# Routing tokens to experts by lists scattered during the conditioning stage, in a fused adapter and mixture-of-experts kernel

## The chip, the cores and the metric

The kernel runs on 1 core of one Trainium2 chip. The metric is the device time of the program in microseconds (us). TensorE (PE), VectorE (DVE), ScalarE (ACT), GpSimd (POOL) and SyncE (SP) each have an instruction queue of their own that runs in order; semaphores couple them. SP starts the plain DMAs, POOL the indirect ones.

## What is computed

4096 tokens of 512 numbers (64 sequences of 64). Each passes a linear layer with a low-rank adapter chosen by its sequence, then two shared experts and the best 2 of 16 routed ones.

```python
def cond(x, W, A, Bm, scalings, adapter_idx):            # x: 64, 64, 512
    H = einsum('btd,od->bto', x, W)
    xa = einsum('btd,brd->btr', x, A[adapter_idx])       # rank 16, 8 adapters
    return H + einsum('btr,bor->bto', xa, Bm[adapter_idx]) * scalings[adapter_idx][:, None, None]

def ffn(x, Wsh_up, Wsh_down, Wrt_up, Wrt_down, W_router):
    xt = x.reshape(B * S, H)
    shared = sum over 2 experts of gelu(xt @ up) @ down  # 512 -> 256 -> 512
    probs = softmax(xt @ W_router)                       # 16 experts
    top_v, top_i = top_k(probs, 2)
    gate = sum(one_hot(top_i) * top_v)
    routed = sum over 16 experts of (gelu(xt @ up) * gate) @ down
    return shared + routed

out = x + ffn(cond(x))
```

## The kernel before

The tokens go in 16 chunks of 256 (NC), each of two tiles of 128 (NT). Where a product is not done in fp32 as it stands, both operands are scaled by powers of two, split into an fp16 part and an fp16 remainder ("high" and "low"), and three fp16 products are summed. Each scale needs the largest magnitude of a tensor over all partitions: DVE reduces along the row, POOL across partitions (`partition_all_reduce`, L517 for weights, L523 for x).

**Conditioning.** One PE step per chunk c (`cond_step`, L1278): adapter products of c (L1238), linear products of tile 0 (L1249), transposes of the conditioned chunk c-1 (L1265), linear products of tile 1, router logits of c-1 (L1274), second adapter products of c (L1257). Chunks 0 and 1 are multiplied whole in fp32 (`whole=True`), since the scales aren't there yet; chunks 2 to 15 use splits: ACT makes the high part of chunk c+1 (`high_x`, L674), DVE the low part (`x_low`, L964). DVE also takes the maximum of the conditioned rows (L898), of the next x (`x_largest`, L947), and the best two logits (`top`, L881). In chunks 1 to 7 DVE searches the 16 lots of expert weights for their maxima as SP loads them (`lot_maxima`, L906: three lots a step in chunks 2 and 3, two later); in steps 4 and 5 it also splits the shared weights. In chunks 8 to 15 ACT and DVE split the weights of two experts a step (`high_routed` L648, `low_routed` L937, both through L641 and L935). SP loads x of chunk c+3 in the step of chunk c, then stores the conditioned rows and their transposes; the loads of further weight lots stand in the same queue behind waits for `lot_max_ready` (`weights_chunk`, L368).

**Sort.** After the last chunk, DVE builds one-hot rows of all 32 tiles (L1051), PE sums them over partitions (`prefix_products`), DVE adds them up over tiles (L1063, L1064), counts tiles per expert, and works out every token's place (L1083 to L1093). The list of tokens by place is found by 64 small matmuls (`inversion_products`, L1313) over one-hot operands which DVE writes two at a time (`places`, L1107 and L1108), in 8 groups. `tok` (L1119) signals `sorted_ready`; only then can POOL gather rows (L574).

Between these stand, in PE's queue, the up and down products of the first 6 chunks of the shared experts (`shared_up` L1327, `shared_down` L1340), in an order written out by hand (L1344 to L1368). Their low parts are made by POOL (`low_condT` L542, `low_hid` L547) from a copy that ACT has scaled a second time (L664, L769). The order ends in the transposes of the first gathered rows, `shared_down(2, 1)`, and the first routed product (`r_up(0)`, L1433).

**Routed stage.** 79 tiles of 128 slots, a pipeline over tiles (`r_round`): transposes, up, down, results stored to `r_dram`. **Late stage.** The other 10 chunks of the shared experts, while POOL gathers back the two routed rows of each token (L608) and DVE weighs and adds them.

Of the kernel before, what the change touches and what calls it, by code (L numbers as in the profile page):

```python
# [5 lines left out]
F32 = mybir.dt.float32  # L6
# [34 lines left out]
GRP = 8  # L41
NG = TT // GRP * K_TOP
# [12 lines left out]
assert EARLY == NC - EARLY - 4 and EARLY <= A_HALF and NC % 4 == 0 and NC == E_RT and EM == HK and NG == 8  # L55


def adaln_moe_kernel(nc, xT, x_rows, idx, WT, AT, BmT, scal, sh_up, sh_dn, rt_w, w_r, out):
# [17 lines left out]
    with ctx:  # L76
# [13 lines left out]
        s_dram = nc.dram_tensor("s_dram", [TOK, H], F32, kind="Internal").ap()  # L90
        r_dram = nc.dram_tensor("r_dram", [NJ * P, H], F32, kind="Internal").ap()
        c_dram = nc.dram_tensor("c_dram", [P], F32, kind="Internal").ap()
# [11 lines left out]
        w_place, a_place = 13, 14  # L104
# [47 lines left out]
        acc0, acc1, pref = carve([((TT, E_RT), F32)] * 3)  # L152

        inv_bufs = carve([((GRP, P), F16), ((GRP, NJ_ALL), F16)] * 2)
        in_part, in_val = inv_bufs[0::2], inv_bufs[1::2]

# [11 lines left out]
        def routed_row(slot, r, t):  # L168
# [8 lines left out]
        iota_p = sb("iota_p", [P, P], F16)  # L177
        iota_j = sb("iota_j", [P, NJ_ALL], F16)
# [11 lines left out]
        lg_c = [sb(f"lg_c{s}", [P, NT, E_RT]) for s in range(2)]  # L190
# [6 lines left out]
        words = TT * E_RT // 2  # L197
        oh = [arena[:, r * words:(r + 1) * words].bitcast(BF16).rearrange("p (t e) -> p t e", t=TT) for r in range(K_TOP + 1)]
        oh_sum = oh.pop()
        at = (K_TOP + 1) * words  # L200
        hi_i, lo_i, hi_f, lo_f = [arena[:, at + n * K_TOP * TT:at + (n + 1) * K_TOP * TT].bitcast(I32 if n < 2 else F32)
                                  .rearrange("p (r t) -> p r t", r=K_TOP) for n in range(4)]
# [5 lines left out]
        pos_f = sb("pos_f", [P, K_TOP, TT])  # L208
        pos = sb("pos", [P, K_TOP, TT], I32)
        past = sb("past", [P, E_RT])  # L210
        tile_col = sb("tile_col", [P, 1])
        tile_e = sb("tile_e", [1, NJ_ALL // 2, 4], I32)
# [7 lines left out]
        expo = sb("expo", [P, len(SCALED)], I32)  # L220
# [7 lines left out]
        x_max = [sb(f"x_max{s}", [P, 1]) for s in range(2)]  # L228
        x_max_all = [sb(f"x_max_all{s}", [P, 1]) for s in range(2)]
# [6 lines left out]
        c_all_row = xam[0][:, 0:P]  # L236

        def col(v, n):
            return v[:, n:n + 1]

# [5 lines left out]
        PRE, TOT, INV, TILE_E = bank[6], bank[7], bank[0], bank[5]  # L246
# [5 lines left out]
        lot_max_ready, largest_ready, reduced, scale_ready, un_ready = (  # L252
            sem("lot_max_ready"), sem("largest_ready"), sem("reduced"), sem("scale_ready"), sem("un_ready"))
# [7 lines left out]
        x_max_found, x_max_ready, x_reduced = sem("x_max_found"), sem("x_max_ready"), sem("x_reduced")  # L261
# [9 lines left out]
        onehot_ready, prefix_ready = sem("onehot_ready"), sem("prefix_ready")  # L271
        shifted_ready, exp_ready = sem("shifted_ready"), sem("exp_ready")
        tile_col_ready, tile_row_ready = sem("tile_col_ready"), sem("tile_row_ready")
        place_ready, place_used, sorted_ready = sem("place_ready"), sem("place_used"), sem("sorted_ready")
# [16 lines left out]
        c_all_stored, c_all_spread = sem("c_all_stored"), sem("c_all_spread")  # L291
# [45 lines left out]
        def _(sp):  # L337
            sp.dma_start(at_in, AT).then_inc(w_adapters, 16)
            sp.dma_start(flat(act_in[0][:]), chunk_T(xT, 0)).then_inc(act_loaded[0], 16)
            sp.dma_start(sc_col[:], scal).then_inc(w_mask, 16)  # L340
            sp.dma_start(idx_b[:], idx.partition_broadcast(P)).then_inc(w_mask, 16)
            for dst, src in ((w_in, WT), (bmt, BmT), (wr, w_r)):
                sp.dma_start(dst, src).then_inc(w_cond, 16)
            sp.dma_start(flat(act_in[1][:]), chunk_T(xT, 1)).then_inc(act_loaded[1], 16)
# [7 lines left out]
            def cond_chunk(i, s, more=True, first=False):  # L352
                c = 2 * i + s
                if more:
                    if first:
                        sp.wait_ge(act_used, 2)
                    else:
                        sp.wait_ge(x_split, c)
                    sp.dma_start(flat(act_in[1 - s][:]), chunk_T(xT, c + 3)).then_inc(act_loaded[1 - s], 16)
                sp.wait_ge(rows_ready, NT * c + NT)  # L360
                sp.dma_start(chunk_rows(xc_dram, c), rows[s][:]).then_inc(rows_stored[s], 16)
                sp.wait_ge(condT_ready, NT * c + NT)
                sp.dma_start(chunk_T(xcT_dram, c), flat(hid[s][:])).then_inc(condT_stored[s], 16)


            def weights_chunk(i, s):
                cond_chunk(i, s, first=(i == 0 and s == 0))
                for r in (2 * s, 2 * s + 1):  # L368
                    n = 4 * i + r
                    if n + 5 == w_place:  # L370
                        sp.wait_ge(act_used, 2)
                        sp.wait_ge(lin_split, 2)
# [28 lines left out]
            load_x(0)  # L401
            cond_chunk(A_HALF - 1, 1, more=False)
            sp.wait_ge(largest_ready, 4)
            sp.dma_start(c_dram.rearrange("(p o) -> p o", o=1), col(largest, C_ALL)).then_inc(c_all_stored, 16)
            sp.wait_ge(c_all_stored, 16)
            sp.dma_start(c_all_row, c_dram.partition_broadcast(P)).then_inc(c_all_spread, 16)
# [8 lines left out]
            sp.wait_ge(cond_ready, TT)  # L415
            for c in range(2):
                next_condT(c)
# [76 lines left out]
        def _(pool):  # L494
# [5 lines left out]
            iota(iota_p[:], P)  # L500
            iota(iota_j[:], NJ_ALL)
            iota(iota_e[:], E_RT)
            nc.gpsimd.iota(tok_no[:], [[P, TT]], base=-TOK // 2, channel_multiplier=1,
# [4 lines left out]
            pool.wait_ge(masks, 3)  # L508
# [5 lines left out]
            def reduce_max(n, a, b):  # L514

                pool.wait_ge(largest_ready, n)
                nc.gpsimd.partition_all_reduce(largest_all[:, a:b], largest[:, a:b], P, RMAX).then_inc(reduced, 1)  # L517

            def x_reduce(c, s):
                pool.wait_ge(x_max_ready, c - 1)
                nc.gpsimd.partition_all_reduce(x_max_all[s][:], x_max[s][:], P, RMAX).then_inc(x_reduced, 1)  # L523

            reduce_max(1, LIN_W, SH_UP)
            reduce_max(2, SH_UP, RT_UP)
            pool.wait_ge(scale_ready, 1)
            for c in range(2, NC):
                x_reduce(c, c % 2)
                if c == NC // 2 + 1:  # L530
                    reduce_max(3, RT_UP, C_ALL)
# [8 lines left out]
            def low_condT(c):  # L540
                pool.wait_ge(condT_half, c + 1)
                nc.gpsimd.tensor_tensor(actT[c % 2][:, 1], by_block(early_condT(c)), actT[c % 2][:, 0],  # L542
                                        ALU.subtract).then_inc(actT_ready, 1)

            def low_hid(c):
                pool.wait_ge(hid_half, c + 1)
                nc.gpsimd.tensor_tensor(hidT[c % 2][:, 1], by_block(tmp[:]), hidT[c % 2][:, 0],  # L547
# [959 lines left out]
```

## Time and profile before

| | us |
|---|---|
| median of 3 runs | 679.23 |
| lowest, highest | 679.11, 682.99 |
| profiled execution, its own time | 681.92 |
| its span | 679.9 |
| PE busy | 627.5 (92%) |
| DVE busy | 457.4 (67%) |
| ACT busy | 327.2 (48%) |
| POOL busy | 222.6 (33%) |

The span runs from the first to the last instruction; the execution's own time has 2.0 us more around it. PE's busy time is modelled, so the order of its pieces and what it waits for say more than its share. "L12" is line 12 of the kernel. In a row of groups the numbers after the bar are total busy us and mean ns of one, then the idle time just before it and what ended that.

### The profile page before, as it was taken

To read this page: it belongs to the slowest core of one execution; us is meant where nothing else is said; L and a number is where in the kernel's file an instruction comes from. 1 tells how busy PE (TensorE), PEld (TensorE's weight loads), DVE (VectorE), ACT (ScalarE), POOL (GpSimd) and SP (SyncE) were. 2 spreads that over 40 slices of the span, in tenths; PEclk is the share of its full clock that TensorE was granted. 3 is DMA by queue.
4 is the path that set the end of the run, shared out by engine and by line. 5 is a ranking of instruction groups with operands and counts; after the bars stand their busy time and mean duration, and the time that the engine had idled before them with its cause. 6 is when DMAs were issued, how large, how long until landed. Compare 5 with 4: busy or idle time off the path is not lost.

```text
span 679.9 us, 13742 instructions
## 1 busy us (share of the span) xinstructions
PE 627.5 (92%) x4115; PEld 428.4 (63%) x4117; DVE 457.4 (67%) x900; ACT 327.2 (48%) x480; POOL 222.6 (33%) x288
## 2 busy tenths in 40 slices
PE   4998999999989758889999999999999999989794
PEld 2465656566657435556777777777777777665561
DVE  2779999999974998525555555555555554688674
ACT  1333224677775743464555555555555554333230
POOL 1000000101012742373333333333333306777771
PEclk9997999999998988999999999999999999999898
DMA  7688994343334312165555555555555539989966
GB/s 275 281 312 286 374 346 168 123 157 142 132 127 128 124 63 93 32 217 171 159 159 169 161 154 159 164 168 157 156 159 167 164 107 377 366 301 362 369 205 248
DMA packets 49765, 135.68 MB, mean 200 GB/s; under 512 B 6160, under 2 KB 6288, under 8 KB 47312
## 3 DMA queue, kind: packets, MB, share of 16 engines
q1 hardware_dynamic: 38304, 97.93, 39.1%
q0 software_dynamic: 11440, 37.50, 20.0%
q8 instruction: 11, 0.18, 0.1%
q14 instruction: 10, 0.08, 0.0%
HBM read 86.38 MB, written 49.02 MB: 199 GB/s over the span
## 4 chain that ended last, share of the span: by engine, by line
PE 53%; DVE 17%; POOL 12%; issue 7%; DMA 7%; ACT 1%; SPq 0%; DVEq 0%; POOLq 0%; ACTq 0%
PE bank L1412 15%; PE bank L1393 14%; POOL rtw L608 9%; PE bank L1249 7%; PE bank L1377 5%; DVE lot_max L906 5%; DMA act_in<-xT 3%; PE bank L1402 2%; PE bank L1327 2%; PE bank L1257 2%; PE bank L1274 2%; DMA region<-xc_dram,slot_idx 2%; PE bank L1238 1%; DVE x_max L947 1%; PE bank L1265 1%
## 5 line engine op out<-in xcount | busy, mean ns | idle before, releaser
L1129 DVE SCALAR_TENSOR_TENSOR region<-bank,scale,region 128x512 f16<-128x512 f32 x79 | 59.2, 751 | 128.7 <-ACT region L809 128.7
L1393 PE MATMUL bank<-rtw,region 128*128 x948 | 116.4, 273 | 0.0
L1412 PE MATMUL bank<-rtw,tmp 128*128 x474 | 115.2, 379 | 0.6 <-DVE tmp L1137 0.6
L1393 PEld LDWEIGHTS bank<-rtw,region 128*128 128x128 f16 x948 | 92.8, 98 | 10.1
L1340 PE MATMUL bank<-shw,hid 128*128 128x512 f16 x384 | 91.3, 397 | 8.3 <-DVE rtw L1193 7.7
L574 POOL DMA_INDIRECT region<-xc_dram,slot_idx x79 | 77.1, 976 | 61.3 <-POOL slot_idx L571 61.3
L1327 PE MATMUL bank<-act_in,shw 128*128 128x256 f16 x768 | 89.4, 277 | 2.9 <-ACT tmp L756 1.7
L1327 PEld LDWEIGHTS bank<-act_in,shw 128*128 128x128 f16 x768 | 75.8, 100 | 16.0 <-ACT tmp L756 2.2
L816 ACT ACTIVATE region<-bank,un_dn 128x512 f32<-128x512 f32 x79 | 54.3, 687 | 57.3 <-PE bank L1412 54.8
L608 POOL DMA_INDIRECT rtw<-r_dram,row_idx x64 | 70.0, 1093 | 27.6 <-issue 14.8
L1340 PEld LDWEIGHTS bank<-shw,hid 128*128 128x128 f16 x384 | 38.4, 102 | 56.4 <-issue 10.0
L1412 PEld LDWEIGHTS bank<-rtw,tmp 128*128 128x128 f16 x474 | 46.3, 98 | 39.2 <-issue 1.3
L805 ACT ACTIVATE tmp<-bank,un_up 128x256 f32<-128x256 f32 x79 | 37.4, 473 | 60.2 <-PE bank L1393 60.2
L1168 DVE SCALAR_TENSOR_TENSOR rtw<-rtw,gate 128x512 f32 (+1 forms) x64 | 45.4, 750 | 15.2 <-DMA rtw<-r_dram,row_idx 13.0
L809 ACT ACTIVATE region<-bank,scale 128x512 f16<-128x512 f32 x79 | 54.1, 687 | 2.2 <-PE bank L1377 2.2
L523 POOL PARTITION_ALL_REDUCE x_max_all<-x_max x14 | 10.7, 763 | 134.9 <-DVE x_max L949 134.9
L1377 PE MATMUL bank<-ident,region 128*128 128x128 f32 x316 | 47.4, 273 | 2.6 <-DMA region<-xc_dram,slot_idx 2.5
L571 POOL COPY slot_idx<-tok 128x1 int32 (+1 forms) x79 | 14.4, 182 | 106.5 <-PE bank L1377 97.0
L756 ACT ACTIVATE tmp<-bank,un_up 128x256 f32<-128x256 f32 x44 | 20.4, 471 | 52.2 <-PE bank L1327 49.9
L641 ACT ACTIVATE rtw<-rtw,scale 128x1024 f16<-128x1024 f32 (+1 forms) x32 | 35.8, 1152 | 17.3 <-DVE rtw L935 15.1
L935 DVE SCALAR_TENSOR_TENSOR rtw<-rtw,scale 128x1024 f16<-128x1024 f32 x32 | 39.6, 1279 | 4.4 <-ACT rtw L641 4.3
L1135 DVE TENSOR_SCALAR tmp<-bank,to_mid 128x256 f16<-128x256 f32 x79 | 38.2, 484 | 6.1 <-PE bank L1402 2.7
(157 smaller groups left out, 910.0 us busy)
## 6 DMA issues: line engine op xcount, KB each, us to landing
r_dram<-region SPq DMA_DIRECT2D x79, 256.0 KB
rtw<-rt_w SPq DMA_DIRECT2D x16, 1024.0 KB, 7.4
act_in<-xT SPq DMA_DIRECT2D x16, 512.0 KB, 3.8
xc_dram<-rows SPq DMA_DIRECT2D x16, 512.0 KB, 3.7
xcT_dram<-hid SPq DMA_DIRECT2D x16, 512.0 KB, 2.8
rtw<-x_rows SPq DMA_DIRECT2D x16, 512.0 KB, 5.4
rtw<-xcT_dram SPq DMA_DIRECT2D x13, 512.0 KB, 6.1
out<-rtw SPq DMA_DIRECT2D x9, 512.0 KB, 5.6
```

Of the source, the lines that this page charges most:

```text
L574: nc.gpsimd.indirect_dma_start(out=xg[s], out_offset=None, in_=xc_dram, in_offset=bass.IndirectOffsetOnAxis(ap=slot_idx[s][:].bitcast(U32) ...
L608: nc.gpsimd.indirect_dma_start(out=routed_row(slot, r, t), out_offset=None, in_=r_dram, in_offset=bass.IndirectOffsetOnAxis(ap=row_idx[slo ...
L809: nc.scalar.activation(xgT[s][:, 0], R_XT[s][:].rearrange("p (k t) -> p k t", k=HK), ACT.Copy, scale=col(scale, C_ALL).bitcast(F32)).then_ ...
L816: nc.scalar.activation(rrow[s], R_DN[s][:], ACT.Copy, scale=col(un_dn, ROUTED)).then_inc(rrow_ready, 1)
L1129: nc.vector.scalar_tensor_tensor(xgT[s][:, 1], R_XT[s][:].rearrange("p (k t) -> p k t", k=HK), col(scale, C_ALL).bitcast(F32), xgT[s][:, 0 ...
L1168: last = nc.vector.scalar_tensor_tensor(y, routed_row(slot, r, t), gate[:, r, bass.ds(c * NT + t, 1)], y, ALU.mult, ALU.add)
L1249: last = mm(COND[NT * s + t][:], act_in[s][:, k, at] if whole else xp[s][:, ap, k, at], w_in[:, k, :] if whole else wt[:, bp, k, :], start ...
L1327: last = mm(UP[em % 2][:, 0:CHUNK], shw[:, e, w0:w0 + P], actT[s][:, xp, k, :], start=(k == 0 and n == 0), stop=(k == HK - 1 and n == 2))
L1340: last = mm(DOWN[t][:], hidT[s][:, xp, em, t * P:(t + 1) * P], shw[:, em // DM, w0:w0 + H], start=(em == 0 and n == 0), stop=(em == EM - 1 ...
L1377: last = nc.tensor.transpose(R_XT[s][:, k * P:(k + 1) * P], xg[s][:, k * P:(k + 1) * P], ident[:])
L1393: last = mm(R_UP[s][:, 0:D], xgT[s][:, xp, k, :], rtw[:, bass.ds(e, 1), w0:w0 + D].rearrange("p a d -> p (a d)"), start=(k == 0 and n == 0 ...
L1412: last = mm(R_DN[s][:], midT[s][:, xp, m, :], rtw[:, bass.ds(e, 1), w0:w0 + H].rearrange("p a h -> p (a h)"), start=(m == 0 and n == 0), s ...
```

## The change

1. **Ranks during conditioning.** `top` now also makes the one-hot rows of its chunk. POOL (`count`) adds up one-hot rows of earlier chunks per partition; PE (`rank_products`) sums them over partitions behind the router's products; DVE (`list_places`, chunk c-2 in step c) reads each token's rank within its expert and forms a slot in a list of 4096 per expert; POOL scatters the token numbers into the lists in DRAM, 4 indirect DMAs of 128 numbers of 4 bytes a chunk (`scatter`, chunk c-3 in step c). The lists are cleared at the start by a DMA of 256 KB.
2. **After the last chunk** DVE only counts tiles, POOL gathers the used pieces of the lists with one indirect DMA, PE transposes them, DVE writes `tok`. The places for the way back (`pos`) are found later. The 64 matmuls with their operands, the prefix sums over tiles, and the two small DMAs for the last maximum are gone.
3. **Maxima over partitions by TensorE.** DVE writes the identity times the column of maxima (`x_diag`, `diag`), PE multiplies ones by it (`spread`, `spread_x`, one matmul of 128 columns each), DVE reduces the 128 columns. For x of chunk c+2 the matmul stands in step c in front of the router's products, which so wait for `x_largest(c+2)`; `x_scales(c+2)` reads it once the logits are there, and stands behind all the step's lots.
4. **Low x on GpSimd.** ACT makes the high part and then scales x in place; POOL subtracts (`low_x`).
5. **One whole fp32 chunk** (chunk 0). Chunk 1 is split and waits for the scales.
6. **Early low parts on DVE.** `low_condT` and `low_hid` of chunks 0 to 6 move from POOL to DVE, straight from the unscaled source; ACT's second scaled copies go.

```diff
@@ sync
+            for c in range(1, 3):
+                sp.dma_start(flat(act_in[c % 2][:]), chunk_T(xT, c)).then_inc(act_loaded[c % 2], 16)
+            sp.wait_ge(masks, 5)
+            sp.dma_start(lists.rearrange("(p a) n -> p (a n)", p=P), lg[:].rearrange("p t e -> p (t e)")).then_inc(lists_cleared, 16)
             sp.dma_start(arrived(0), sh_up).then_inc(w_shared, 16)
             sp.dma_start(spare, sh_dn).then_inc(w_shared, 16)
-            sp.wait_ge(act_used, 1)
-            sp.dma_start(flat(act_in[0][:]), chunk_T(xT, 2)).then_inc(act_loaded[0], 16)
...
@@ gpsimd
+            def low_x(c, s):
+                pool.wait_ge(x_half, c)
+                nc.gpsimd.tensor_tensor(un_cond[s][:], x_unscale[s][:].bitcast(F32), col(unscale, LIN_W).bitcast(F32), ALU.mult)
+                nc.gpsimd.tensor_tensor(xp[s][:, 1], act_in[s][:], xp[s][:, 0], ALU.subtract).then_inc(x_split, 1)
...
+            low_x(1, 1)
+            pool.wait_ge(lists_cleared, 16)
+            for c in range(1, NC):
+                if c + 1 < NC:
+                    low_x(c + 1, (c + 1) % 2)
+                if c > 2:
+                    scatter(c - 3)
+                count(c - 1, (c - 1) % 2)
+            scatter(NC - 3)
+            count(NC - 1, 1)
+            scatter(NC - 2)
+            scatter(NC - 1)
+            pool.wait_ge(list_ready, 1)
+            pool.wait_ge(scattered, 16 * K_TOP * TT)
+            nc.gpsimd.indirect_dma_start(
+                out=tokT, out_offset=None, in_=lists,
+                in_offset=bass.IndirectOffsetOnAxis(ap=list_i[:].bitcast(U32), axis=0),
+            ).then_inc(tokT_loaded, 16)
...
@@ vector, a step of chunks 2 to 7 (x_low has left the steps of 8 to 15 too, which end in the same three calls)
-            def search_step(i, s, lots, masked=False):
+            def search_step(i, s, lots):
                 c = 2 * i + s
-                if not masked:
-                    mask_xa(c, s)
+                mask_xa(c, s)
                 row_max(c - 1, 1 - s)
-                x_low(c + 1, 1 - s)
...
+                x_largest(c + 2, s)
+                for at in lots:
                     lot_maxima(at)
                 x_scales(c + 2, s)
-                for at in lots[2:] if masked else lots[1:]:
-                    lot_maxima(at)
                 top(c - 1, 1 - s)
+                list_places(c - 2, s)
...
@@ vector, behind the last chunk
+            link(nc.vector.tensor_reduce(col(largest, C_ALL), c_chunk[:], AX_X, ALU.max))
+            spread_out(C_ALL, C_ALL + 1)
+            early_low_condT(1)
+            early_low_hid(0)
+            find_all(C_ALL, C_ALL + 1)
             top(NC - 1, 1)
...
+            list_places(NC - 2, 0)
+            early_low_condT(2)
+            scales(4, C_ALL, C_ALL + 1)
+            result_scales(SH_REST, C_ALL, SH_UP, SH_DN)
+            result_scales(ROUTED, C_ALL, RT_UP, RT_DN)
+            early_low_hid(1)
+            list_places(NC - 1, 1)
...
+            early_low_condT(3)
+            early_low_hid(2)
             dve.wait_ge(tile_row_ready, 1)
...
+            dve.wait_ge(inverted, 1)
+            nc.vector.tensor_copy(tok[:], INV[:, 0:NJ_ALL]).then_inc(sorted_ready, 1)
+            early_low_condT(4)
+            early_low_hid(3)
...
@@ tensor
+            def rank_products(k, s):
+                pe.wait_ge(counted, k + 1)
+                mm(PLACE, lower[:], oh_sum[s][:], start=True, stop=False)
+                return mm(PLACE, ones[:], earlier[s][:], start=False, stop=True)
...
+                if peaks_of is not None:
+                    pe.wait_ge(x_all_found, peaks_of - 1)
+                    spread_x(peaks_of)
+                if ranks_of is not None:
...
+                    rank_products(ranks_of, 1 - s)
...
             shared_up(0, 0, first=True)
-            router_products(NC - 1, 1)
+            pe.wait_ge(logit_copied, NC - 1)
+            spread(4, 1)
+            router_products(NC - 1, 1, ranks_of=NC - 2)
             shared_up(0, 1)
-            prefix_products()
+            last_rank_products()
             shared_down(0, 0, first=True)
             shared_up(1, 0)
             tile_expert_product()
             shared_down(0, 1)
+            token_transpose()
             shared_up(1, 1)
-            inversion_products(0)
...
```

## Rows read from the trace of the kernel before

**Rows 1.** The page's chain that ended last: shares by engine, by line.
```profile
PE 53%; DVE 17%; POOL 12%; issue 7%; DMA 7%; ACT 1%; SPq 0%; DVEq 0%; POOLq 0%; ACTq 0%
PE bank L1412 15%; PE bank L1393 14%; POOL rtw L608 9%; PE bank L1249 7%; PE bank L1377 5%; DVE lot_max L906 5%; DMA act_in<-xT 3%; PE bank L1402 2%; PE bank L1327 2%; PE bank L1257 2%; PE bank L1274 2%; DMA region<-xc_dram,slot_idx 2%; PE bank L1238 1%; DVE x_max L947 1%; PE bank L1265 1%
```

**Rows 2.** Stretches: busy us (count) by engine, granted clock, DMA share, GB/s.
```profile
133.60:187.90 54.30, 54.30 (x323) 34.84 (x321) 52.40 (x116) 40.76 (x48) 5.42 (x5) 1.00 0.37 138
202.60:296.30 93.70, 76.41 (x526) 49.65 (x526) 67.50 (x201) 50.41 (x70) 39.52 (x24) 0.90 0.32 102
250.00:262.00 12.00, 8.40 (x41) 3.78 (x42) 9.51 (x35) 1.85 (x4) 3.27 (x2) 0.63 0.00 0
296.30:553.20 256.90, 253.72 (x1865) 189.95 (x1864) 133.49 (x232) 140.92 (x234) 91.77 (x153) 1.00 0.55 162
```

**Rows 3.** Timeline: where steps 2, 4, 8, the first shared and routed products start.
```profile
16.55 2.62 ACT L668 ACTIVATE region<-rtw,scale 128x2048 f16<-128x2048 f32 x2 [14.46 <-DVE scale L920]
...
37.00 0.27 PE L1238 MATMUL bank<-tmp,region 128*128 128x256 f16 x1
...
64.55 0.27 PE L1238 MATMUL bank<-tmp,region 128*128 128x256 f16 x1
...
110.14 0.27 PE L1238 MATMUL bank<-tmp,region 128*128 128x256 f16 x1
...
202.63 0.40 PE L1327 MATMUL bank<-act_in,shw 128*128 128x256 f16 x1
...
296.30 0.93 PE L1393 MATMUL bank<-rtw,region 128*128 x7
```

**Rows 4.** The chain in order of time, one PE step (start, us, what).
```profile
133.61 1.31 PE bank L1238 x12
134.92 2.59 PE bank L1249 x12
137.51 0.87 PE bank L1265 x8
138.38 2.59 PE bank L1249 x12
140.97 1.69 PE bank L1274 x16
142.66 1.81 PE bank L1257 x4
```

**Rows 5.** Groups of instructions by line, whole span.
```profile
L906 DVE TENSOR_REDUCE lot_max<-rtw 128x2 f32<-128x2048 f32 x16 | 36.3, 2278 | 0.0
L947 DVE TENSOR_REDUCE x_max<-act_in 128x1 f32<-128x1024 f32 x14 | 17.0, 1213 | 6.1 <-DMA act_in<-xT 6.1
L964 DVE SCALAR_TENSOR_TENSOR tmp<-act_in,x_scale,tmp 128x1024 f16<-128x1024 f32 x7 | 8.9, 1277 | 0.0
L674 ACT ACTIVATE tmp<-act_in,x_scale 128x1024 f16<-128x1024 f32 x7 | 8.0, 1147 | 17.6 <-DVE x_scale L958 17.6
L914 DVE TENSOR_REDUCE largest_all<-xam 128x1 f32<-128x128 f32 x1 | 0.3, 285 | 0.0
L893 DVE CAST chosen<-best_i_c 128x4 f32<-128x4 uint32 x16 | 4.6, 284 | 0.5
```

**Rows 6.** Timeline: GpSimd's subtraction beside small VectorE instructions.
```profile
200.36 2.13 POOL L542 TENSOR_TENSOR act_in<-tmp,act_in 128x1024 f16<-128x1024 f32 x1 [25.34 <-ACT tmp L664]
200.51 2.00 DVE L893 CAST chosen<-best_i_c 128x4 f32<-128x4 uint32 x1
```

**Rows 7.** GpSimd's indirect DMAs, one line: ns min/median/max.
```profile
L608 POOL DMA_INDIRECT rtw<-r_dram,row_idx x64: 942/966/1886, 562.9 to 664.0; - x64
```

**Rows 8.** DMA issues by line: KB each, us to landing.
```profile
sc_col<-scal SPq DMA_DIRECT2D x1, 0.5 KB, 3.3
c_dram<-largest SPq DMA_DIRECT2D x1, 0.5 KB, 10.2
```

**Rows 9.** Timeline at the end of the sort.
```profile
281.86 0.24 DVE L1119 TENSOR_SCALAR tok<-bank 128x80 int32<-128x80 f32 x1 [0.26 <-PE bank L1313]
```

More of the change, by code:

```diff
@@ new lines, in scatter @@
+            def scatter(k):
+                pool.wait_ge(slot_ready, k + 1)
+                for r in range(K_TOP):
+                    for n in range(NT * k, NT * k + NT):
+                        nc.gpsimd.indirect_dma_start(
+                            out=lists.rearrange("a (n o) -> (a n) o", o=1),
+                            out_offset=bass.IndirectOffsetOnAxis(ap=pos[:, r, n:n + 1].bitcast(U32), axis=0),
+                            in_=tok_no[:, n:n + 1], in_offset=None,
+                        ).then_inc(scattered, 16)
@@ new lines, in _ @@
+            early_low_condT(4)
+            early_low_hid(3)
+            dve.wait_ge(scattered, 16 * K_TOP * TT)
+            for r in range(K_TOP):
+                link(nc.vector.tensor_tensor(acc, iota_e[:].unsqueeze(1).to_broadcast([P, TT, E_RT]),
+                                             chosen[:, r, :].unsqueeze(2).to_broadcast([P, TT, E_RT]), ALU.is_equal))
+                link(nc.vector.tensor_tensor(acc, acc, start_s[:].unsqueeze(1).to_broadcast([P, TT, E_RT]), ALU.mult))
+                link(nc.vector.tensor_reduce(starts[:, r, :], acc, AX_X, ALU.add))
@@ L1127, in low_xgT @@
+            nc.vector.tensor_tensor(pos[:], starts[:], rank[:], ALU.add).then_inc(pos_ready, 1)
+            early_low_condT(5)
+            early_low_hid(4)
+            link(nc.vector.tensor_tensor(lg[:], lg[:], best[:, :, 0:1].to_broadcast([P, TT, E_RT]), ALU.subtract))
+            nc.vector.tensor_tensor(best[:, :, 1:2], best[:, :, 1:2], best[:, :, 0:1], ALU.subtract).then_inc(shifted_ready, 1)
+            early_low_hid(5)
+            early_low_condT(6)
             def low_xgT(j, s):
@@ L1294, in _ @@
             pe.wait_ge(lin_split, 2)
[L1295 to L1304 removed]
+            adapter_inputs(1, 0, 1)
@@ new lines, in _ @@
+            cond_products(1, 1, 0, first=True)
+            cond_transposes(0, 0, first=True)
+            cond_products(1, 1, 1, first=True)
+            pe.wait_ge(x_all_found, 2)
+            spread(2, 2)
+            router_products(0, 0, peaks_of=3, first=True)
+            adapter_products(1, 1)
+            pe.wait_ge(all_found, 2)
+            cond_step(2, 1, 0, second=True)
+            cond_step(3, 1, 1)
+            with pe.Fori(2, A_HALF // 2) as i:
+                for s in range(2):
+                    cond_step(2 * i + s, i, s)
@@ new lines, in _, with last_rank_products @@
+            for s in range(2):
+                cond_step(NC // 2 + s, A_HALF // 2, s, middle=s == 0)
+            with pe.Fori(A_HALF // 2 + 1, A_HALF - 1) as i:
+                for s in range(2):
+                    cond_step(2 * i + s, i, s)
+            for s in range(2):
+                cond_step(NC - 2 + s, A_HALF - 1, s, more=False)
+            cond_transposes(NC - 1, 1)
+            def last_rank_products():
+                pe.wait_ge(logit_copied, NC)
+                pe.wait_ge(all_found, 4)
+                pe.wait_ge(rank_read, NC - 1)
+                rank_products(NC - 1, 1)
+                mm(TOT, ones[:], earlier[1][:, 1, :], start=True, stop=False)
+                mm(TOT, ones[:], oh_sum[1][:, 1, :], start=False, stop=True).then_inc(ranked, 1)
```

476 lines of the change are left out of this document (233 added, 243 removed).

## The prediction

> **What bounds the kernel now.** I read the page's chain first [rows 1]: PE's two routed products are its largest lines, but DVE has 17% of it, and POOL's and the lots' lines stand there too, so the stages have different limits. The stretches say where [rows 2]. The routed stage, 296.30 to 553.20, is PE throughout at full clock; the change leaves its loop as it is, and the late stage too. The stretch before it, 202.60 to 296.30, holds the sort: PE is busy 76.41 of 93.70 us at a granted clock of 0.90, and in 250 to 262 the clock is 0.63 of 2.4 GHz, that is, part of it at the 1.2 GHz level, after PE had stood idle for DVE. In the conditioning steps of 133.6 to 187.9 PE is full, and DVE is nearly so (52.40 of 54.30). So the question is by how much the first routed product, at 296.30 [rows 3], moves; everything behind it moves along. That product stands at the end of a fixed order on PE, which begins at 202.63.
>
> **Part 1: the sort behind the last chunk (what goes).** Half a shared chunk, up or down, is 48 products of 256 columns or 24 of 512, the same column count. Twelve products of 512 columns take 2.59 us in an undisturbed step [rows 4], so half a chunk takes 5.2. In PE's new order stand 12 halves before `r_up(0)`: 62.4 us. To these come the last router products (1.7), 8 transposes of gathered rows (0.9, as the eight at 137.51), and about 1.6 for the new small products and the first gelu, on which the third block of the first half waits: 66.6 us. Now it is 93.7. The difference, 27, is what PE loses to DVE's writing of one-hot operands, to POOL's low parts and to the lower clock.
>
> Does the rest keep up? With U for the start of the first half: ACT needs for a chunk four gelus, a high hidden part, a high input and two row copies, under 6 us of 10.4. `top(15)` ends near U+10, for the router stands behind the first half and DVE first makes two low parts of 1.28 (L964's shape [rows 5]). The second half ends at U+12.9, `last_rank_products` at U+13.2; `list_places(15)` is held back by `early_low_hid(1)` to U+17. The scatters of the last chunk are four indirect DMAs at 1.0 us [rows 7] and their semaphore time: issued by U+22. DVE's twenty or so small links give the list numbers at about U+21. Scatter landed at U+25, gather issued and landed at U+29. PE reaches `token_transpose` behind the second chunk's first down half, at U+29.0: a dead heat, against `tok` at 281.86 now [rows 9], which is U+79. DVE's low parts for chunks 3 to 5 then come 2 to 5 us ahead of PE. I add 2 us for small stalls: 68.5 instead of 93.7, **-25.2 us**.
>
> The scatter is the unknown here; this trace has none. Nearest are: issue 966 ns, up to 1886 [rows 7]; landing 3.3 us for 128 elements of 4 bytes when little is under way, 10.2 us for such a store behind four transfers of 512 KB [rows 8]. I take 3.5 and 4 us for scatter and gather, since at U+22 the queues are light (mean DMA share 0.32 in that stretch [rows 2]). With 10.2 for the scatter and 6 for the gather, `tok` is 9 us later, and so is PE.
>
> **Part 2: the head.** The first scales are ready at 16.5 (ACT's first split [rows 3]). Now chunk 1's maximum, three diagonals and a round trip over PE stand before them: some 2.7 us, 19.2. ACT splits the linear weights (2.62), makes chunk 1's high part and scales it in place, 2 times 1.15 [rows 5], 24.1; POOL subtracts, 2.13 [rows 6], after DVE's split of the linear weights: 27.2. PE, done with chunk 0 before that, waits. Step 1 as fp16 then takes 7.4 us to its router (1.31+2.59+0.87+2.59 [rows 4]), 34.6. The router now needs chunk 3's diagonal, and DVE has in front of it the row maximum (1.2, the shape of L947), the two shared weight maxima (2 times 2.28 [rows 5]) and the maximum itself (1.21): 37.1. Router 1.7 and adapter 1.8 end at 41.0. Step 2 started at 37.00 [rows 3]: **+4.0**. What the fp16 products of chunk 1 save on fp32 is in this, since it starts late anyway.
>
> **Part 3: steps 2 to 7.** DVE sets the pace: from step 4 to step 8 it is 45.6 us, 11.4 a step [rows 3], over PE's 10.9 [rows 4]. It loses `x_low`, 1.28, and its scalar, hardly anything from start to start (1.3 in all), and gains the diagonal (0.25 and a link of 0.2), the reduction of 128 columns (0.285 [rows 5] and 0.17 for the link), and three links of `list_places`, 0.8; `top` loses three copies and gains a wider comparison, even. Net 0.4 a step (small DVE links by estimate: 0.17 for the instruction, as the undisturbed casts of rows 5, and as much again for the semaphore), and I take 0.55, as the order puts the lots ahead of `x_scales`, and the next x load stands on SP behind a wait for them: 6 steps, **+3.3**. Step 8 starts at 117.5 instead of 110.14.
>
> **Part 4: steps 8 to 15.** At step 8 PE waits in its own queue for three diagonals of the routed scales, which DVE can only write after step 7, 2.7 us; before, DVE alone stood for that. I take **+2.1**. Then PE is full: one product of 128 columns and two of 32 a step, at 0.1 us each, as the sixteen of 16 columns in 1.69 [rows 4]: 6 steps, **+1.7**. DVE comes to 10.5 (52.40 in five steps [rows 2]) - 1.3 + 1.7 = 10.9 us, just under PE's 11.1. At the end ACT has one scaled copy less before the last rows: **-1.0**.
>
> **Part 5: the shared port.** While POOL's subtraction ran (2.13 us), DVE's cast of 4 elements took 2.00 us [rows 6]; the other 15 took 0.17 ((4.6 - 2.0)/15 [rows 5]). There are 15 `low_x` in the new conditioning. By my placing, `low_x(c+1)` runs 3.8 to 6.0 us into step c, when DVE is at its two row maxima. These have one input, and that they aren't held up is assumed, not shown. So most of it is hidden: 0.16 us a chunk, **+2.4**. The bounds are 0 and 2.13 a chunk.
>
> The Trainium skill says why ("SBUF — State Buffer", section "SBUF: two separate sides"): the port pair that VectorE and GpSimd share is an exclusive lock for the whole instruction, which a VectorE instruction takes with two SBUF inputs against a GpSimd one that reads SBUF. The trace agrees, 2.00 us against 0.17. By that rule alone `low_routed`, with two inputs, would be held up each time it meets `low_x`: this speaks against the change, and is the first rival.
>
> **The sum.** Conditioning: 4.0 + 3.3 + 2.1 + 1.7 - 1.0 + 2.4 = +12.5. Sort: -25.2. Together -12.7: the profiled execution's 681.92 would be 669.2, and the median of the runs, 679.23, which stands 2.7 under it, becomes **666.5 us**. That is 1.9% less; a measurement of this kernel can tell about 1% (6.8 us) from no change.
>
> **Rivals.**
> *The port eats it (slower; 0.12).* `low_x` lies not under the reductions but across `low_routed` and `low_shared`. For it: DVE is at 97% in steps 9 to 14 [rows 2], so nothing else hides it. Against it: ACT's high parts come after cond_T there, and DVE has to wait for them anyway. The full price is 15 times 2.13, 32 us, in place of my 2.4: 696. It turns the change slower from 1.0 us a chunk on (12.7/15 more than I took).
> *The lists come late (0.13).* Landings as in the upper bound: +9, 675.5; what speaks for it is the store of 10.2 us. If each scatter's issue costs 1.9 us, as the longest of rows 7, POOL, with 2.3 for `low_x`, 4 times 2.2 and by estimate 1.6 for `count` a step, is over PE's 11.1 by 1.6 a step and comes to about the same range, 685 (within this chance).
> *Conditioning hardly pays (0.20).* DVE's added links fall into waits for loads (L947 waited 6.1 us for x [rows 5]) and for ACT; only the head's 4 us stay: 666.5 - 8.5 = 658.
> *The sort wasn't what held PE.* Then nothing is gained and +12.5 stays: 692; PE's order shows no other reason for 17 idle us, so 0.03.
> The forecast itself: 0.52.
>
> **Range and chances.** 8 in 10 lie between 653 (conditioning free, sort -26.5) and 682. Faster by over 1% (under 672.4): my case and the third rival, with part of the second, 0.79. Within 1%: 0.09. Slower by over 1%: 0.12.
>
> **What would show it.** Right: step 2's first product near 41, step 8's near 117, the first shared one near 215, `tok` some 30 us after that, `r_up(0)` near 283.5, granted clock 1.00 in between, steps of 11.1 to 11.3 us in 9 to 15. Wrong: DVE instructions of about 2 us beside L-lines of `low_x` in steps 8 to 15 (first rival); PE idle before the token transpose (second); steps over 11.5 us with POOL at over 10 busy. If the token list is there before U+25 and still `r_up(0)` is later than U+70, DVE's new low parts are late, a step that I costed at 2 us.

## The result, and the profile after

The changed kernel takes **707.75 us** (median of 4 runs, 701.67 to 716.01) against 679.49 for the kernel before beside it: ratio 1.0374, 95% interval 1.0275 to 1.0473. It is slower, outside the range of 653 to 682. The ratio leaves out the longest of the four runs, 716.01 us, which is in the slow state; it is the profiled one (span 714.3), and without it the median is 704.32, so that differences taken from 707.75 below would be 3.4 us smaller.

Where the stages begin, first and last start in us, as the lines' own view of the changed kernel gives them (L1281 is the adapter product that opens a step, L1418 the first shared product, L1476 the first routed one); they answer to [rows 3]:

```profile
L1281 PE MATMUL bank<-tmp,region x84: 272/273/307, 40.3 to 228.1; 128*128 128x256 f16 x84
L1418 PE MATMUL bank<-act_in,shw x768: 272/273/421, 251.0 to 696.6; 128*128 128x256 f16 x192
L1476 PE MATMUL bank<-rtw,region x948: 272/273/273, 332.2 to 589.2; 128*128 x190
```

Step 2 starts at 40.3, 0.7 us from the forecast, so the head is as worked out. But the first shared product comes at 251.0 instead of 215, and `r_up(0)` at 332.2 instead of 283.5. Conditioning lost 48.4 us against before (forecast 12.5); the sort stage takes 81.2 us instead of 93.7 (forecast 68.5). Everything behind is as it was.

Stretches of the changed kernel (busy us and count of PE, PEld, DVE, ACT, POOL; granted clock, DMA share, GB/s; the last two are the stages of [rows 2]):

```profile
80.00:100.00 20.00, 3.30 (x18) 3.25 (x18) 5.02 (x5) 0.00 (x0) 1.89 (x2) 0.54 1.05 122
82.00:95.00 13.00, 0.00 (x0) 0.00 (x0) 0.09 (x1) 0.00 (x0) 0.19 (x1) 0.50 1.17 126
120.00:140.00 20.00, 12.96 (x55) 8.25 (x54) 8.38 (x22) 4.08 (x6) 6.03 (x10) 0.66 1.06 141
251.00:332.20 81.20, 71.49 (x469) 47.70 (x466) 32.77 (x86) 37.79 (x58) 31.20 (x35) 0.89 0.56 132
332.20:589.00 256.80, 254.45 (x1872) 190.60 (x1871) 134.61 (x235) 141.73 (x235) 89.79 (x152) 1.00 0.54 160
```

From 82 to 95 the compute engines stand all but still and the 16 DMA engines are full, at 126 GB/s (the view's share can pass 1, since it counts a packet's whole time where the packet starts). The kernel before had the same fullness in 80 to 100, at three times the rate:

```profile
80.00:100.00 20.00, 18.57 (x107) 11.53 (x106) 19.73 (x39) 5.93 (x9) 0.35 (x1) 1.00 0.94 363
```

So the DMA engines are as busy while they move a third of the bytes. The page's part on DMA of the changed kernel (packets, MB, share of 16 engines; KB each, us to landing):

```profile
q1 hardware_dynamic: 38160, 98.12, 49.2%
xc_dram<-rows SPq DMA_DIRECT2D x16, 512.0 KB, 8.9
xcT_dram<-hid SPq DMA_DIRECT2D x16, 512.0 KB, 7.3
act_in<-xT SPq DMA_DIRECT2D x15, 512.0 KB, 8.8
lists<-tok_no,pos POOLq DMA_INDIRECT x64, 8.7
```

and of the kernel before:

```profile
q1 hardware_dynamic: 38304, 97.93, 39.1%
act_in<-xT SPq DMA_DIRECT2D x16, 512.0 KB, 3.8
xc_dram<-rows SPq DMA_DIRECT2D x16, 512.0 KB, 3.7
xcT_dram<-hid SPq DMA_DIRECT2D x16, 512.0 KB, 2.8
```

The plain transfers are the same in number and size, and take over twice as long. Who waits for them? The waits of the changed kernel between 40 and 200 us (us in total, times, longest), and the timeline around the first long stop:

```profile
DVE x_max L989 <- DMA act_in<-xT: 44.9, 6, 19.2
PE bank L1313 <- DVE tile_e L994: 36.6, 5, 17.7
```

```profile
77.39 1.00 POOL L541 DMA_INDIRECT lists<-tok_no,pos  x1 [0.15 <-issue]
...
79.03 0.91 SPq L361 DMA_DIRECT2D act_in<-xT  x1
...
81.23 0.96 POOL L541 DMA_INDIRECT lists<-tok_no,pos  x1 [0.30 <-issue]
94.91 1.22 DVE L989 TENSOR_REDUCE x_max<-act_in 128x1 f32<-128x1024 f32 x1 [19.19 <-DMA act_in<-xT]
```

Four scatters of 512 bytes each (L541) are issued from 77.4 to 82.2; an x chunk is issued among them at 79.0, behind two weight lots of 1 MB, and lands at 94.9; DVE's row maximum (L989) starts only then, and behind it the diagonal, the router on PE and the whole step. The chain that ended last has such transfers too. Its three longest:

```profile
68.00 26.89 DMA act_in<-xT
...
126.12 24.79 DMA act_in<-xT
...
251.81 22.12 DMA xcT_dram<-hid
```

The last of the three is the store of the last conditioned chunk's transposes (their buffer is called `hid`). The next load waits for it on SP, ACT waits for that load, and PE stops at 283.9 in the third shared chunk:

```profile
283.94 5.30 PE L1418 MATMUL bank<-act_in,shw 128*128 128x256 f16 x24 [4.17 <-ACT tmp L771]
```

An earlier stop of 5.5 us, up to 263.9, comes from a load that is late in the same way (ACT waits 7.1 us for `rtw<-xcT_dram`, DVE for ACT, PE for DVE). These two stops are 9.7 us of the sort stage. None of the four rivals names this. The list is late too (GpSimd's gather waits 5.9 us for the last scatter), but that stands behind the 35 us that are lost by then. What is left is that the scatters slow the core's other transfers, or that the order of the loads does it. The experiments take these apart.

### The profile page after: what moved, and what is told of

The parts are those of the page before. It is cut to its first block, busy times and chain, and to the rows that moved or that the text cites. A ratio compares the mean times of both kernels' runs of the same rounds, so it can differ in the third digit from the quotient of the medians.

```text
span 714.3 us, 13732 instructions
## 1 busy us (share of the span) xinstructions
PE 637.6 (89%) x4120; PEld 435.1 (61%) x4121; DVE 423.9 (59%) x805; ACT 331.9 (46%) x483; POOL 303.2 (42%) x432
## 3 DMA queue, kind: packets, MB, share of 16 engines
q1 hardware_dynamic: 38160, 98.12, 49.2%
## 4 chain that ended last, share of the span: by engine, by line
PE 57%; DMA 17%; POOL 9%; issue 7%; DVE 6%; ACT 2%; SPq 1%; POOLq 0%; DVEq 0%; ACTq 0%
PE bank L1495 14%; PE bank L1476 14%; DMA act_in<-xT 10%; POOL rtw L622 8%; PE bank L1292 5%; PE bank L1460 5%; PE bank L1300 3%; PE bank L1339 3%; PE bank L1418 3%; DMA xcT_dram<-hid 3%; PE bank L1431 3%; PE bank L1281 3%; PE bank L1485 2%; DMA rtw<-r_dram,row_idx 1%; DVE x_max L989 1%
## 5 line engine op out<-in xcount | busy, mean ns | idle before, releaser
L1476 PE MATMUL bank<-rtw,region 128*128 x948 | 116.4, 273 | 0.0
L1418 PE MATMUL bank<-act_in,shw 128*128 128x256 f16 x768 | 91.8, 282 | 9.7 <-DVE act_in L1094 5.5
L1476 PEld LDWEIGHTS bank<-rtw,region 128*128 128x128 f16 x948 | 92.7, 98 | 10.1 <-issue 0.2
L1431 PE MATMUL bank<-shw,hid 128*128 128x512 f16 x384 | 88.8, 389 | 8.2 <-DVE rtw L1236 8.2
L1418 PEld LDWEIGHTS bank<-act_in,shw 128*128 128x128 f16 x768 | 77.3, 101 | 24.0 <-DVE act_in L1094 5.6
L541 POOL DMA_INDIRECT lists<-tok_no,pos x64 | 65.8, 1027 | 21.3 <-issue 16.4
L817 ACT ACTIVATE tmp<-bank,un_up 128x256 f32<-128x256 f32 x79 | 37.5, 474 | 61.0 <-PE bank L1476 61.0
L699 ACT ACTIVATE rows<-bank,un_cond 128x512 f32<-128x512 f32 x30 | 20.4, 685 | 84.2 <-PE bank L1300 83.8
L1292 PE MATMUL bank<-region,arena 128*128 128x512 f16 x192 | 45.1, 386 | 0.0
L989 DVE TENSOR_REDUCE x_max<-act_in 128x1 f32<-128x1024 f32 x15 | 18.2, 1214 | 45.0 <-DMA act_in<-xT 44.9
```

Source lines behind the costliest of these rows:

```text
L541: nc.gpsimd.indirect_dma_start(out=lists.rearrange("a (n o) -> (a n) o", o=1), out_offset=bass.IndirectOffsetOnAxis(ap=pos[:, r, n:n + 1]. ...
L1292: last = mm(COND[NT * s + t][:], x_first[:, k, at] if whole else xp[s][:, ap, k, at], w_in[:, k, :] if whole else wt[:, bp, k, :], start=( ...
L1418: last = mm(UP[em % 2][:, 0:CHUNK], shw[:, e, w0:w0 + P], actT[s][:, xp, k, :], start=(k == 0 and n == 0), stop=(k == HK - 1 and n == 2))
L1431: last = mm(DOWN[t][:], hidT[s][:, xp, em, t * P:(t + 1) * P], shw[:, em // DM, w0:w0 + H], start=(em == 0 and n == 0), stop=(em == EM - 1 ...
L1476: last = mm(R_UP[s][:, 0:D], xgT[s][:, xp, k, :], rtw[:, bass.ds(e, 1), w0:w0 + D].rearrange("p a d -> p (a d)"), start=(k == 0 and n == 0 ...
```

## The experiments

All ratios stand against the kernel before on the same chip, whose medians in the three groups of runs were 681.54 (e1 to e4), 681.46 (e5, e7, e8, e9) and 682.10 us (e6, e10, e11, e12). The edits are shown shortened.

### Without the scatters, and beside the kernel before

```diff
 e1:
-  nc.gpsimd.indirect_dma_start(out=lists..., in_=tok_no[:, n:n + 1])
-  pool.wait_ge(scattered, 16 * K_TOP * TT)
-  nc.vector.tensor_copy(tok[:], INV[:, 0:NJ_ALL])
+  nc.vector.tensor_scalar(tok[:], INV[:, 0:NJ_ALL], part_f[:], None, ALU.add)
 e4, e5, on the kernel before, in GpSimd's loop behind x_reduce(c), c from 2:
+  for n in range(4):
+      nc.gpsimd.indirect_dma_start(out=lists, in_=tok_no[:, n:n + 1],
+          index place_i[:, 4 * c - 8 + n])
 e4: place_i[p, j] = 128 * j + p      e5: place_i[p, j] = j + 64 * p
 both: GpSimd waits for all 56 scatters behind the loop
```

> The changed kernel without its 64 scatters; the token list is filled with partition numbers instead, so each routed tile gathers rows 0 to 127, and the routing list is not computed; all other instructions stay. Theory S (the scatters slow the core's plain DMAs in the conditioning): the median lands of the x chunks and of the stored rows are back near those of the kernel before (3.8 and 3.7 us instead of 8.8 and 8.9), the first shared product starts near 215 us instead of 251, and the total is 662 to 672 us. Rival O (the order of the loads, the wait of SP, or the shared port cost the time, and the scatters are innocent): x still lands late, the first shared product stays beyond 240, total over 695 us.

Measured: **662.94 us**, ratio 0.9726 (0.9695 to 0.9756). First shared product at 216.9, `r_up(0)` at 283.1. The stored rows land as before (median 3.3 us); the x chunks do not come back to 3.8 us, as I had expected, but only to 6.3.

> The kernel before plus 56 scatters, four a chunk from chunk 2 on, each 128 numbers of 4 bytes into 128 neighbouring places of a scratch array; nothing waits for them before the first shared sum. Theory S: the conditioning loses 15 to 45 us, x lands at 7 us or more, total 695 to 725 us. Rival O: POOL has room for four issues of 1 us a chunk, total within 3 us of the kernel before (677 to 683).

Measured: **752.32 us**, ratio 1.1011 (1.0952 to 1.1071), beyond my 725. 28 KB in 56 scatters cost 70.8 us in a kernel that has nothing else of the change. Its page:

```profile
q1 hardware_dynamic: 38304, 97.93, 51.2%
rtw<-rt_w SPq DMA_DIRECT2D x16, 1024.0 KB, 18.3
act_in<-xT SPq DMA_DIRECT2D x16, 512.0 KB, 16.3
```

> The kernel before plus the same 56 scatters of 128 numbers as in e4, but each number 256 bytes from the next one of its scatter. Theory N (neighbours written within one scatter stall the core's transfers): within 4 us of the kernel before, 678 to 686 us, x chunks landing at 4 to 5 us (median). Rival A (any 4-byte write does it, where it goes plays no part): as e4, over 740 us.

Measured: **683.17 us**, ratio 1.0031 (1.0003 to 1.0059): 1.7 us. Its page:

```profile
q1 hardware_dynamic: 38304, 97.93, 39.4%
rtw<-rt_w SPq DMA_DIRECT2D x16, 1024.0 KB, 7.4
act_in<-xT SPq DMA_DIRECT2D x16, 512.0 KB, 4.5
```

Here, as DMAs, bytes, POOL's work and issue times are alike, the places of the 4-byte writes decide between 70.8 us and 1.7. One more thing stands in e5: its four scatters of a chunk write four neighbouring places for each partition, and by the end all 64 places of each 256 bytes are written. Neighbours that *successive* scatters write do no harm that shows; those of one and the same scatter do.

### How far apart, how wide

```diff
 e2: out=wide (rows of 16 floats), in_=iota_e[:]           64 bytes a write
 e3: pos * 16     e6: pos * 8     e7: pos * 2              4 bytes a write, 64, 32, 8 bytes apart
 all: tok[:] is filled with partition numbers
```

> The changed kernel, whose 64 scatters write 64 bytes per token instead of 4 into a scratch array of 4 MB (the list stays as cleared and the token list is filled with partition numbers). Same number of DMAs, of descriptors and of issues; only the size and spacing of each write differ. If it is the small size of a write (4 bytes, neighbours in one 64-byte line or not): as without scatters, total 662 to 675 us. If it is the number of descriptors or the way an indirect DMA goes (software queue, 128 rows each): as the changed kernel, over 695 us, x landing at 8 us or more.

> The changed kernel, whose 64 scatters write their 4 bytes per token 64 bytes apart in a scratch array of 4 MB (one more small DVE instruction a chunk; the token list is filled with partition numbers). If neighbouring 4-byte writes of different DMA engines into one line are what stalls: as without scatters, 662 to 675 us. If any 4-byte write stalls, wherever it goes, or any indirect DMA: as the changed kernel, over 695 us.

> As e3 and e7, with the places 32 bytes apart (4-byte writes; the token list is filled with partition numbers). Between 8 bytes (683.1) and 64 bytes (666.8). If the unit in which neighbours stall is 32 bytes or less: 664 to 669 us. If it is 64 bytes, two places share a unit: 670 to 678 us.

> As e3, but the places are 8 bytes apart instead of 64 (as for these runs, the token list is filled with partition numbers). Theory N with a unit of 64 bytes or more: still several numbers of one expert in a unit, so most of the loss stays, 690 to 710 us. If only writes that touch within a few bytes count: as e3, about 667 us.

Measured: e2 **666.73 us** (ratio 0.9792, 0.9759 to 0.9826), e3 **666.76** (0.9764, 0.9703 to 0.9825), e6 **667.43** (0.9804, 0.9752 to 0.9855), e7 **683.08** (1.0014, 0.9991 to 1.0038). The number of writes is that of the changed kernel in all four, and so are the issues: neither 64 indirect DMAs nor 4-byte writes as such cost more than 5 us over e1. In e7 a loss stays, of 16.3 us over e3, though I had expected more of it, 690 us or above.

### Whole kernels with another list

```diff
 e8 (e11 with 4 for 8, and so 16 bytes):
-  lists = [E_RT * LIST, P] F32
+  lists = [E_RT * LIST * P, 8] I32                  32 bytes a place
-  in_=tok_no[:, n:n + 1]                            scatter
+  in_=tok_w[:, n:n + 8]                             the number first, 32 bytes a write
-  out=tokT, in_=lists                               gather, 512 bytes a partition
+  out=slots, in_=lists as rows of 128 places        gather, 4 KB a partition
+  tok_pick = slots[:, 0:8 * P:8] & (TOK - 1); tokT = tok_pick      DVE, ahead of the transpose
 e9 (places dense, as in the changed kernel):
+  pos = pos & 0xFF80 | (pos << 4) & 0x70 | (pos >> 3) & 15         five DVE instructions a chunk
+  a copy on DVE turns the gathered rows back
```

> The changed kernel, whole, with a list of 32 bytes per place (the scatter writes 32 bytes, the number first), cleared by one transfer of 2 MB in place of 256 KB, gathered as 4 KB a partition. Two more small DVE instructions in all. If 32 bytes per write are enough: 668 to 678 us, of which 3 to 6 us are the clearing, since the head is full of transfers. If the unit that stalls is 64 bytes: 685 to 700 us.

> As e8, whole, with 16 bytes per place and per write, and 1 MB cleared. If the stall comes from writes smaller than some unit of 32 bytes that touch each other: 670 to 685 us. If 16 bytes per write are enough: 663 to 667 us, for half of the clearing is saved too.

> The changed kernel, whole, with the 4-byte list kept as dense as it is, but the rank in a tile turned round before the scatter (its three low bits become the upper ones), so eight consecutive ranks lie 64 bytes apart, and a copy on DVE turns the gathered rows back. Five more small DVE instructions a chunk. Theory N says that the neighbours of one scatter are what counts (some eight tokens per expert in one of 128 tokens and one choice): the conditioning is free of the stall, total 668 to 676 us with about 3 us for DVE. Rival D (a dense list is slow however it is written, since lines are rewritten again and again): over 695 us.

Measured: e8 **665.67 us** (ratio 0.9783, 0.9734 to 0.9832), e11 **671.45** (0.9843, 0.9797 to 0.9890), e9 **682.19** (1.0016, 0.9979 to 1.0053). e8 computes all that the changed kernel does, is 42.1 us faster than it and 2.2% faster than the kernel before (2.4% in its repetition e12, below). It came out 2.3 us under my range: the larger clearing costs less than I had put on it. e9 misses my range: the turn takes away more than half of the loss, not all of it.

How crowded each list is can be counted. With the router's choices on the reference's inputs (arithmetic, no measurement) one scatter of 128 numbers has so many writes, in the mean, that fall into a unit of 32 bytes in which the same scatter has already written:

| kernel | bytes from place to place | such writes of 128, unit 32 bytes (64 bytes) | us over its like without them |
|---|---|---|---|
| e4 | 4, all in a row | 112 (120) | 70.8, over the kernel before |
| changed | 4 | 87 (99) | 42.1, over e8 |
| e7 | 8 | 63 (87) | 16.3, over e3 |
| e9 | 4, turned | 32 (35) | 16.5, over e8, with five DVE instructions a chunk in it |
| e11 | 16 | 31 (63) | 5.8, over e8 |
| e6, e8 | 32 | 0 (31) | 0.7 over e3; e8 is the base |
| e2, e3, e5 | 64 and more | 0 (0) | bases; e5 1.7 over before |

The loss vanishes where the third column is 0. By a unit of 64 bytes e6 and e8 would have shared units as often as e11 has by 32, and they lose nothing. By one of 16 bytes e11 would lose nothing, and it takes 6.0 us more than e12 on the same chip. So places 32 bytes apart are enough here and 16 are not quite.

Above 0 this count doesn't give the size of the loss: e9 has half of e7's shared writes and loses as much. Its five more DVE instructions a chunk are the smaller part of it, for the transfers themselves are late. The waits of DVE for x, from 40 to 200 us, in e9, e7, e11 and e8:

```profile
DVE x_max L997 <- DMA act_in<-xT: 24.6, 5, 6.5
DVE x_max L991 <- DMA act_in<-xT: 23.0, 6, 6.0
DVE x_max L994 <- DMA act_in<-xT: 12.4, 4, 5.7
DVE x_max L994 <- DMA act_in<-xT: 10.8, 5, 5.7
```

So 13.8 of e9's 16.5 us are waits for x beyond e8's. A closer look at the distance is nearer the order of the losses: within a unit of 16 bytes, e4 has 96 shared writes, the changed kernel 63, e7 31, e9 27, e11 none. It seems that writes 4 or 8 bytes apart weigh more than those 16 apart; that is read from these few runs, in which the width of a write and the work of DVE change too, and was not tried by itself.

The Trainium skill has two sentences beside this. "DMA: Bandwidth & Descriptors", section "Specifications", says that a transfer below 512 bytes makes the DMA engine read, modify and write. Alone that doesn't sort these runs: e2's and e8's writes of 64 and 32 bytes, and e3's of 4, are all far below 512 and cost at most 4 us over e1. "Collectives: The Full Stack", section "Rules for kernel authors", asks for buffers of collectives aligned to 32 bytes, since that "Prevents HW read-modify-write"; 32 bytes is also the distance at which the loss vanishes in these runs. That a read before each partial write is what makes the neighbours wait for each other is the likely reading, and no trace here shows it.

### The rest of the change: the low x on GpSimd

```diff
 e10, on e8:
-  nc.gpsimd.tensor_tensor(xp[s][:, 1], act_in[s][:], xp[s][:, 0], ALU.subtract)
+  nc.vector.tensor_tensor(xp[s][:, 1], act_in[s][:], xp[s][:, 0], ALU.subtract)   behind row_max
```

> e8 with the low part of x back on DVE, in the place where the kernel before had it (behind the row maximum), and nothing of it on GpSimd. My sum has +2.4 us for the shared port and takes 1.3 us a chunk off DVE. If DVE's 1.3 us a step are what count (steps 2 to 7, where DVE sets the pace, and 8 to 15, where it is 10.9 against PE's 11.1): 5 to 15 us slower than e8. If the port eats the gain (the first rival of the prediction): the same as e8 or faster.

> e8 once more, unchanged, beside e10 on the same chip: 664 to 668 us.

Measured: e10 **672.45 us** (ratio 0.9866, 0.9828 to 0.9905), e12 **665.48** (0.9760, 0.9720 to 0.9799). The move of the subtraction is worth 7.0 us. The stretch 140 to 190 of e8 and of e10:

```profile
140.00:190.00 50.00, 50.00 (x310) 32.57 (x309) 44.92 (x103) 40.02 (x46) 35.13 (x49) 1.00 0.39 138
```

```profile
140.00:190.00 50.00, 48.94 (x279) 29.58 (x277) 47.84 (x119) 37.40 (x42) 23.19 (x42) 0.97 0.40 138
```

In e8 PE is full at 1.00; in e10 DVE has 47.84 of 50 and PE 48.94 at 0.97. And the shared port? e8's low parts of routed weights, 32 in steps 8 to 15, and its subtractions on GpSimd (ns min/median/max):

```profile
L982 DVE SCALAR_TENSOR_TENSOR rtw<-rtw,scale x32: 1277/1282/1286, 132.0 to 213.0; 128x1024 f16<-128x1024 f32 x32
L523 POOL TENSOR_TENSOR arena<-act_in,arena x8: 2128/2142/2632, 23.3 to 195.6; 128x1024 f16<-128x1024 f32 x8
L999 DVE TENSOR_SCALAR tile_e<-ident,x_max x15: 285/286/606, 16.0 to 186.4; 128x128 bf16<-128x128 f32 x15
```

None of the 32 is stretched, but none of them meets a subtraction either: they wait for ACT, and start 0.5 us or more after it has ended, as in step 10:

```profile
151.14 2.13 POOL L523 TENSOR_TENSOR arena<-act_in,arena 128x1024 f16<-128x1024 f32 x1
154.02 2.48 DVE L982 SCALAR_TENSOR_TENSOR rtw<-rtw,scale 128x1024 f16<-128x1024 f32 x2 [0.63 <-ACT rtw L660]
```

DVE's row maxima do run beside the subtraction and keep their time (L994 took 1.20 us at 90.68, beside the subtraction of 90.49), which Part 5 had assumed. Among DVE's other instructions before 215 us one stands out, a diagonal of 606 ns instead of 286, beside that same subtraction. One with two inputs in SBUF does meet GpSimd, behind the last chunk, beside GpSimd's sum of 2.37 us, and is held up:

```profile
240.68 3.48 DVE L1104 SCALAR_TENSOR_TENSOR hid<-tmp,to_mid,hid 128x1024 f16<-128x1024 f32 x1 [3.74 <-ACT hid L787]
240.69 2.37 POOL L575 TENSOR_TENSOR rows<-rows,rtw 128x1024 f32<-128x1024 f32 x1
```

DVE's instruction takes 3.48 us instead of 1.28. The first rival had the mechanism right and the place wrong. The instruction here has two inputs in SBUF, the case on which the first rival stood; the cast of 2.00 us in [rows 6], which Part 5 gave as agreeing, has one, and so didn't show that case. GpSimd is held up as well: beside DVE's low part of shared weights (2.40 us from 86.89) its sum of 16 numbers (L538, at 87.22) takes 2.15 us, where it takes 0.22 alone; what that costs was not tried.

## Why the prediction was wrong

The step that failed is the scatter's cost in Part 1, and with it what Part 3 and Part 4 left out. The prediction gave the scatters an issue time on GpSimd, 1.0 us, and a landing time, 3.5 to 10.2 us, and took both for their whole cost. It never asked what they do to the transfers beside them. The landing times came from [rows 8], a load of 3.3 us and a store of 10.2, and the second was put down to the four transfers of 512 KB ahead of it. The trace of before says otherwise. The store is issued at 203.87 and landed at 214.09, and in most of that time nothing else was moving (the last two numbers of the stretch are DMA share and GB/s):

```profile
208.00:214.00 6.00, 5.46 (x39) 4.44 (x37) 3.24 (x11) 3.77 (x5) 4.19 (x2) 0.77 0.00 0
```

It writes 128 numbers of 4 bytes side by side, as each of e4's scatters does. So a sign of the cost stood in the row that was used; that the crowding made this store slow was not tried by itself. Nor was there a rival for it: the second had the lists late, which is what a slow scatter does to its own reader, not to x.

The other steps can be read from e8, which differs from the changed kernel in the list alone. Where its stages begin:

```profile
L1289 PE MATMUL bank<-tmp,region x84: 272/273/273, 40.7 to 192.8; 128*128 128x256 f16 x84
L1426 PE MATMUL bank<-act_in,shw x768: 269/273/283, 215.7 to 645.7; 128*128 128x256 f16 x192
L1484 PE MATMUL bank<-rtw,region x948: 272/273/273, 283.0 to 539.8; 128*128 x190
```

and steps 8 to 10 in its timeline:

```profile
120.97 1.47 PE L1289 MATMUL bank<-tmp,region 128*128 128x256 f16 x12
124.66 0.23 PE L1326 MATMUL bank<-tile_e,ones 128*128 128x128 bf16 x1 [2.22 <-DVE tok L947]
...
136.27 1.47 PE L1289 MATMUL bank<-arena,region 128*128 128x256 f16 x12
...
147.33 1.47 PE L1289 MATMUL bank<-tmp,region 128*128 128x256 f16 x12
```

| step of the prediction | forecast | e8 | verdict |
|---|---|---|---|
| Part 2, step 2 starts | 41.0 (its own terms give 40.6) | 40.7 (changed kernel 40.3) | right |
| Part 3, steps 2 to 7 against before | +3.3, and 1.0 of Part 5 | 80.2 - 73.1 = +7.1 | too small by 2.8 |
| Part 4, steps 8 and 9 | +2.1, and a part of +1.7 | 26.4 - 23.5 = +2.9 | right |
| Part 4, steps 10 to 15 and the tail | rest of +1.7, -1.0 | 68.4 - 69.0 = -0.6 | right; steps of 11.06 us, forecast 11.1 to 11.3 |
| Part 5, shared port | +2.4 | one instruction, 0.3 us | too large by 2.1 |
| conditioning, first shared product | 215 | 215.7 | right by luck: Part 3's and Part 5's errors cancel |
| Part 1, sort stage | 68.5 | 283.0 - 215.7 = 67.3 | right |
| median | 666.5 | 665.67 | right, in part by that luck |

Part 3's error: x chunks land later. In e8 DVE waits 10.8 us for them in five places; median from issue to landing is 7.2 us, and in e1, without any scatter or larger clearing, 6.3, against 3.8 before. Up to 200 us only 4.7 us of that are more than the 6.1 of [rows 5]; the rest, by difference, is DVE's new small instructions. The new order puts loads of weights ahead of x, which I had seen and put at 0.15 us a step. That the order is the reason was not tried by itself.

Part 1 in e8's sort stage, whose busy shares stand against [rows 2]:

```profile
215.70:283.00 67.30, 66.35 (x468) 45.09 (x467) 35.74 (x88) 38.08 (x58) 32.42 (x35) 1.00 0.50 165
```

PE is busy 66.35 of 67.30 us at full clock; the stall for DVE's one-hot operands and the lower clock of 250 to 262 are gone; the stage is 26.4 us shorter, where the forecast had 25.2. The dead heat of token list and PE came too:

```profile
236.40 1.38 POOL L546 DMA_INDIRECT lists<-tok_w,pos  x1 [0.30 <-issue]
...
239.69 0.98 POOL L566 DMA_INDIRECT arena<-lists,list_i  x1 [1.91 <-DMA lists<-tok_w,pos]
...
244.94 0.33 PE L1414 MATMUL bank<-ident,arena 128*128 128x128 f32 x1 [0.54 <-DVE arena L1162]
...
245.31 0.24 DVE L1164 CAST tok<-bank 128x80 int32<-128x80 f32 x1 [0.42 <-PE bank L1414]
```

The last scatter has landed 1.9 us after its issue ended (forecast 3.5), the list is in at about 244.4 and the token list is there at 245.3, U + 29.6, where the forecast had "some 30"; PE waited 0.54 us. In the changed kernel the gather waits `5.92 <-DMA lists<-tok_no,pos`, and the token list comes at U + 44.

So the sum came out for a kernel whose scatters disturb nobody, and the changed kernel is not that kernel. Between the medians of e8 and of it lie 42.1 us; between the two profiled executions 49.2, of which 35.3 are lost before the first shared product (251.0 - 215.7) and 13.9 in the sort stage (81.2 - 67.3).

## What to carry to other kernels

A small DMA has three costs: its issue, its landing, and what it takes from the transfers beside it; the third counted most here, and it shows as a DMA share near 1.0 at a third of the usual GB/s. When one scatter writes entries smaller than 32 bytes and its indices are likely to be neighbours, as ranks in a list are, give each entry 32 bytes (or put them 32 bytes apart), even if the array has to be cleared and read at eight times the size: in this kernel some 2 MB more of clearing and reading was far cheaper than 32 KB of crowded writes. Before costing an operation by the nearest row of a trace, ask in what the row differs in its addresses, not only in bytes and count.

## What the runs showed that I had not expected

- 56 scatters of 512 bytes each, 128 places in a row, cost 70.8 us (e4); the same 256 bytes apart cost 1.7 us (e5).
- Writes of one scatter do no harm when their places are 32 bytes apart (e6, e8), and still a little at 16 (e11); neighbours written by successive scatters do none that shows (e5).
- A single store of 128 neighbouring numbers took 10.2 us in the kernel before, with no other transfer under way for most of it.
- The harm falls on plain transfers of another queue: x chunks of 512 KB from 3.8 to 16.3 us in e4, with 16 engines shown as nearly full (share 0.98 from 100 to 140, at 198 GB/s).
- Open: which part of the way holds the writes up; by what rule the loss grows with the number and closeness of the neighbours (e9 loses as much as e7 with half the shared units of 32 bytes); and whether the order of the loads makes x late in e1 and e8.
